# Fusion kernel, 16 batches: the 14 middle batches written out one by one, in place of a loop of 14 passes

## The reference, cut to what matters

```
h = concat(x @ W_tok + position_table, text_embedding(x_txt))   # 1024 + 77 rows of 128
y = layernorm(h)
for each of 8 heads (64 wide): q, k, v = y @ wq, y @ wk, y @ wv
    o = softmax(q k^T / 8) v
h = h + concat(o) @ head_kernel
f = layernorm(h) * ln_scale + ln_bias
out = h + shared_ffn(f) + sum over the 2 chosen of 8 experts (weight_e * expert_e(f))
```

## Time and profile before

| | |
|---|---|
| median of 3 runs | 4751.49 us |
| the profiled execution | 4757.83 us |
| its span, first to last instruction | 4756.0 us |
| instructions | 93178 |
| PE busy | 4492.7 us, 94% |
| DVE, ACT, POOL busy | 68%, 48%, 62% |
| mean granted TensorE clock | 0.979 |

### The profile page before, as it was taken

How to read it: one execution, slowest core, us unless ns; L and a number is a source line. 1 busy time by engine, 2 the same in 40 slices (tenths; PEclk the granted TensorE clock), 3 DMA queues, 4 the chain that set the end, 5 groups by cost and what they waited for, 6 DMA issues and landing times.

```text
span 4756.0 us, 93178 instructions
## 1 busy us (share of the span) xinstructions
PE 4492.7 (94%) x26597; PEld 3327.0 (70%) x26597; DVE 3214.1 (68%) x7726; ACT 2300.4 (48%) x5640; POOL 2948.3 (62%) x1803
## 2 busy tenths in 40 slices
PE   5999999999999999999999999999999999999996
PEld 3667767677676776767677676776767777677765
DVE  5557667676675776667676675776667676676744
ACT  2555545445544545545545444555445455454441
POOL 0776666666666666666666666666666666666661
PEclk7999999999999999999999999999999999999998
DMA  2111111111101111111111111011011111111000
GB/s 52 34 33 40 31 30 39 36 28 33 43 26 39 29 32 41 29 34 39 33 31 33 34 34 39 25 33 44 24 39 38 30 34 33 31 37 38 19 19 18
DMA packets 157061, 159.01 MB, mean 33 GB/s; under 512 B 66576, under 2 KB 148359, under 8 KB 156551
## 3 DMA queue, kind: packets, MB, share of 16 engines
q1 hardware_dynamic: 156551, 152.68, 13.2%
HBM read 59.63 MB, written 19.65 MB: 17 GB/s over the span
## 4 chain that ended last, share of the span: by engine, by line
PE 77%; DMA 7%; issue 5%; DVE 4%; ACT 3%; POOL 2%; SPq 1%; DVEq 0%; ACTq 0%; POOLq 0%
PE o_ps L791 21%; PE work L688 12%; PE scores L772 11%; PE scores L774 10%; PE work L747 8%; PE work L680 4%; DMA q_b<-max_rows 4%; DMA sums<-inverse_rows 2%; PE work L708 2%; PE work L699 2%; PE work L731 2%; PE work L736 1%; DMA inverse_rows<-inv_cols 1%; ACT probs L877 1%; DVE part_max L935 1%
## 5 line engine op out<-in xcount | busy, mean ns | idle before, releaser
L1165 POOL TENSOR_TENSOR sums<-sums,probs 128x736 f32<-128x736 f32 (+3 forms) x1344 | 2363.2, 1758 | 840.4 <-ACT probs L877 783.1
L877 ACT ACTIVATE probs<-scores 128x368 f32<-128x368 f32 (+3 forms) x3456 | 1460.3, 475 | 1595.9 <-PE scores L774 1535.4
L935 DVE TENSOR_REDUCE part_max<-work 128x1 f32<-128x368 f32 (+3 forms) x3456 | 1655.9, 530 | 448.8 <-PE work L688 438.5
L772 PE MATMUL scores<-q_a,k_a 128*128 128x368 f32 (+3 forms) x3456 | 1193.9, 345 | 143.3 <-DMA q_b<-max_rows 62.7
L791 PE MATMUL o_ps<-probs,values 128*64 128x368 f32 (+1 forms) x6912 | 1224.8, 490 | 1.5 <-ACT probs L877 0.2
L774 PE MATMUL scores<-q_b,k_b 128*128 128x368 f32 (+3 forms) x3456 | 1146.0, 332 | 0.0
L688 PE MATMUL work<-k_a,q_a 128*128 128x368 f32 (+3 forms) x3456 | 928.5, 352 | 8.8 <-DMA q_a<-q_b 8.1
L791 PEld LDWEIGHTS o_ps<-probs,values 128*64 128x64 f32 (+1 forms) x6912 | 453.8, 139 | 541.1 <-issue 449.2
L772 PEld LDWEIGHTS scores<-q_a,k_a 128*128 128x128 f32 (+1 forms) x3456 | 635.5, 184 | 269.8 <-issue 128.1
L688 PEld LDWEIGHTS work<-k_a,q_a 128*128 128x128 f32 (+1 forms) x3456 | 594.7, 185 | 234.3 <-issue 209.2
L774 PEld LDWEIGHTS scores<-q_b,k_b 128*128 128x128 f32 (+1 forms) x3456 | 638.8, 185 | 17.4 <-issue 4.2
(11 more groups left out here) (183 smaller groups left out, 4499.2 us busy)
## 6 DMA issues: line engine op xcount, KB each, us to landing
sums<-inverse_rows SPq DMA_DIRECT2D x192, 184.0 KB
k_a<-k_a SPq DMA_DIRECT2D x128, 184.0 KB, 2.7
q_a<-q_b SPq DMA_DIRECT2D x128, 184.0 KB, 2.7
k_a<-k_a SPq DMA_DIRECT2D x64, 183.0 KB, 2.7
q_a<-q_b SPq DMA_DIRECT2D x64, 183.0 KB, 2.7
resid_rows<-heads_t SPq DMA_DIRECT2D x16, 576.0 KB, 6.1
h_out<-resid_rows SPq DMA_DIRECT2D x16, 576.0 KB, 8.2
heads_t<-in_pe_table_dram SPq DMA_DIRECT2D x16, 512.0 KB
```

Of the source, the lines that this page charges most:

```text
L772: nc.tensor.matmul(o, k_a[p % 2][i][:, t * P:t * P + n], q_a[p % 2][i][:, c0:c0 + cw], start=True, stop=False)
L877: nc.scalar.activation(probs[0:n, slot(s), i, 0:cw], scores[0:n, h % SB, 0:cw], ACT.Exp, scale=DH ** -0.5).then_inc(probs_ready, 1)
L935: nc.vector.tensor_reduce(part_max[0:n, i * IMG + j if j < IMG else 2 * IMG + i, c:c + 1], w[0:n, 0:keys], AX.X, ALU.max).then_inc(drained ...
L1165: nc.gpsimd.tensor_tensor(acc, acc, probs[0:n, slot(s), :, 0:cw], ALU.add).then_inc(sums_done, 1)
```

## The change

In `run`, the hardware loop becomes a Python loop. The middle 14 batches stand in each engine's stream one after the other, b is an integer in all of them, so the waits of these batches are on constants, and the counting, comparing, branching and register arithmetic fall away. The work, its order on each engine and all buffers stay.

```
         iteration(pro, 0, -1)
         iteration(first, 0, 0)
-        with eng.Fori(1, B - 1) as b:
+        for b in range(1, B - 1):
             iteration(loop, b - 1, b)
         iteration(last, 0, B - 1)
         iteration(epi, 0, B)
```

## The result

The changed kernel takes 4717.7 us, the median of 5 runs (4715.6 to 4730.7), against 4752.3 (4749.5 to 4755.1, 5 runs) for the one before on the same chip: 0.9933 of its time, 95% interval 0.9921 to 0.9944. It is 34.6 us faster where 19.7 were forecast. The profiled execution took 4715.6 us, its span 4713.6. All runs behind the medians here are in the same state but one, a slow run of the last experiment (9373 us), which is left out.

The account below looks back on a forecast made before the run. The prediction took TensorE, busy 94% of the span, and its pauses as the bound. Passages -34.3 us and constants +14.6 us summed to -19.7 us, from 4751.5 to 4732 us; overall range 4705 to 4754 us.

Parts of the forecast that it names:

- The 13 pauses at the branch: TensorE's waits for "issue" when the loop branches back, 43.6 us together, 3.35 us each, would go.
- Rival E: Between batches: the pause isn't the branch's and remains in another form; only +14.6 us stay, 4766 us; chance 0.03.
- The passage's value, 14.50: Each of 13 passages between batches falls from 17.14 to 14.50 us, copy late, clock falling one in three: 34.3 us saved.
- rival B: Passages between batches: the q_a copy isn't late, all go like that into batch 1; -43 us, 4708 us; chance 0.13.
- C: Passages between batches: the copy is late and the clock falls each time; -5 us, 4746 us; chance 0.18.
- Register arithmetic at nothing: On all five engines, removing the loop's register operations gains nothing, since the engines' queues cover them.
- Rival G: Second half of a batch: removing register arithmetic gains back what constants cost there; -34.3 us alone, 4717 us; chance 0.04.
- Constants, 1.04 us a batch,: ScalarE's separate semaphore waits hand exponentials over 0.08 us later: 1.04 us a batch, 14.6 us for 14 batches.
- The doubling: The 0.52 us lost over 49 steps doubled to 1.04 us for a whole batch, whose other half couldn't be compared.
- Steps 53 to 55 unchanged: TensorE's step 53 pause, about 2.1 us, clock falling in 3 of 15 batches, got no term in the sum.
- Rival D: ScalarE's separate waits ahead of exponentials cost more than the branches, from 2.45 us a batch; +26 us, 4778 us; chance 0.09.
- Rival F: Straight-line batches: the instruction stream can't keep up, 267 us for some 230 exposed blocks; 4999 us; chance 0.03.

Follow-up runs that it names:

- the last experiment: The loop kernel before the change, with ScalarE's wait for scores_ready written ahead of those for probs_used and sums_done: 1.0109, 4807.2 us.
- The kernel of two passes: Against the kernel before: loop kept on every engine, but of 2 passes with 7 batches written out in each, registers kept: 0.9950, 4725.3 us.
- the small load: Against the kernel before: middle batches written out on TensorE only, residual load cut to 32 bytes a partition, h_out zeroed once: 0.9909, 4707.9 us.
- TensorE alone: Against the kernel before: middle batches written out on TensorE only, the other four engines keep the loop: 1.0019, 4759.3 us.
- VectorE, GpSimd and SyncE: Against the kernel before: middle batches written out on these three engines, TensorE and ScalarE keep the loop: 1.0007, 4753.8 us.
- TensorE and SyncE: Against the kernel before: middle batches written out on these two engines, the other three keep the loop: 1.0000, 4753.6 us.
- The reordered waits: The changed kernel with ScalarE's wait for scores_ready written first in its step; against the kernel before 0.9912, 4708.7 us, and again 0.9912, 4708.3 us.
- ScalarE alone: Against the kernel before: middle batches written out on ScalarE only, the other engines keep the loop: 1.0072, 4785.9 us.
- the second time: The changed kernel, unedited, run once more beside the version with reordered waits; against the kernel before 0.9928, 4718.7 us.
- TensorE and ScalarE alone: Against the kernel before: middle batches written out on these two engines, the other three keep the loop: 1.0015, 4755.8 us.

## Why the prediction was right, and where it was not

*The 13 pauses at the branch* were right: the 13 waits for "issue" and the branch rows are gone, with the lower clock that followed them. The two windows that the prediction shows for that clock, 0.81, are among the five lowest; in the other eight it was 0.90. The trace of the kernel before also shows what a pause holds. In each of the 13, one 16 KB packet of the instruction fetch on q8 starts 0.9 to 1.6 us behind the start of TensorE's branch and ends at 1.9 to 2.6; the branch that falls through has none. The window of the branch into batch 14, 4082.42 to 4086.13, of the view of the DMA queues:

```profile
q8 instruction: 1, 0.02, 2.2%
```

By the Trainium skill, "Runtime: NRT & Kernel Launch", section "Instruction fetch mechanics", a taken branch out of the fetched window waits for a fetch of the target's code; the packets agree. Rival E (4766) falls.

*The passage's value, 14.50, failed.* It was 12.47, so 4.66 a passage were saved instead of 2.64, 26 us in 13. The step that failed is "I take the wait as there, since batches 2 to 14 follow a batch with feed-forward and output store, as batch 15 does and batch 1 doesn't". I read the passage into batch 15 as a sample of the changed kernel, and it was none for two reasons. Its tail, the end of batch 14, is loop code with registers; with constants everywhere the residual load goes out 0.64 us earlier against the same matmul. And its load was the slowest of the 16, 9.5 us, where I took the median, 8.2, for it; into batch 15 it takes 9.4 us in the changed kernel too, in the 13 others 8.0 to 8.2. With both gone the copy is in time, or late by 0.42 us at most. The kernel of two passes shows the forecast's passage, 13.87, where the tails keep their registers; the small load shows that it is the load that holds the copy up. Mechanism and place of the danger were right, that it would be met was not: this part went as rival B had it (4.45 a passage), and C (4746) falls. That the time still lay in the range is in part luck: the passages gave 26 us more than forecast, and 13 us of costs that the forecast had too low took half of it back.

*Register arithmetic at nothing* holds for the body: about 0 in the steps of the kernels with TensorE alone and with VectorE, GpSimd and SyncE. Rival G falls. Not at the passage: there the tails' register code is worth 1.40 us a passage through the load. No one engine has it all. Into batch 15, where all these kernels have a straight passage, the load goes out at +0.01 us with every tail on registers, at +0.03 with TensorE written out, at +0.08 with VectorE, GpSimd and SyncE, at -0.24 with TensorE and SyncE, at -0.30 with ScalarE, with or without TensorE, and at -0.64 only with all five.

*Constants, 1.04 us a batch,* had the right mechanism and too small a size: 18.9 / 13 = 1.45 us. The reordered waits show the mechanism, ScalarE alone shows the engine. The doubling was at fault: the first half cost (1.7 + 4.6) / 13 = 0.48, near the 0.52 taken, but the second (6.8 + 5.8) / 13 = 0.97, twice as much. Why isn't shown: TensorE's waits for exponentials, at L772 and L791 together, rose by about as many in the first half (192 in 13 batches) as in the second (187).

*Steps 53 to 55 unchanged*, a term that the sum left out without a word, failed. The three steps cost 0.59 us a batch more: in batches 2 to 14 the clock fell in 4 (3 the second time) instead of 1, and in two batches TensorE's pause itself was 3.0 and 3.2 us in place of 2.1. Why, and whether the constants have to do with it, isn't shown. With passages and constants this makes -60.6 + 18.9 + 7.7 = -34.0, where the same terms of the forecast for 13 batches are -34.3 + 13.5 = -20.8.

*Rival D* (more than 2.45 us a batch) falls by its own mechanism, the constants' 1.45. Its sign, that a batch without its passage grows by more than 2.4 us, came near: 26.6 / 13 = 2.05, for the falls at steps 53 to 55 are in it. With TensorE and ScalarE alone it was 36.5 / 13 = 2.8, and the kernel was slower than before. *Rival F* falls: it needed 267 us.

Open: why the load into batch 15 takes longer than the others, and about half of the 8.4 us at the ends of the span, which lie in batches 0 and 15, where both kernels have the same code.

## What to carry to other kernels

A boundary that a trace seems to show "already unrolled" is a sample only if both sides of it are unrolled, and one sample needs its own rows: compare its transfer with the others before taking their median for it. Look at the code that issues the transfers, not only at the engine that pauses. Removing a pause on the bounding engine is worth only what the next transfer allows; here that hung on one load on a shared queue, its issue and its length. Of the variants that wrote out only some engines and computed everything, none was faster than the loop. When an instruction has more waits than it can hold, look at which wait the compiled instruction carries, and try an order in which it is the one that ends last. The same edit that gained 10 us with constants cost 56 in the loop.

## What the runs showed of the hardware

- A taken branch back over a long body cost TensorE 3.5 us at the median, with one 16 KB instruction packet on q8 inside it each time; to take away VectorE's, GpSimd's and SyncE's gained nothing (1.0007). The Trainium skill, "Advanced Engine Details and Errata", section "Control Flow Timing", has about 108 ns for a compare-and-branch; TensorE's taken ones took 30 times that here, VectorE's 63 ns, and the measurement decides.
- A separate semaphore instruction of 38 ns, if it holds the wait that ends last, delays the exponential behind it by 0.08 us; the register operations in its place by 0.15.
- The pause at steps 53 to 55 is 1.8 to 3.2 us in all kernels, mostly 2.1. In batches 2 to 14 the clock fell there in 1 batch before, in none with VectorE, GpSimd and SyncE written out, in 4 and 3 in the two runs of the changed kernel, and in 5 to 12 in all others, at some 1.5 to 2 us each; there these steps cost 11 to 19 us in all. In the first run of the changed kernel it didn't fall at the two longest pauses, 3.0 and 3.2 us, but at five shorter ones of 2.1 to 2.6. What decides it isn't shown.
- The same 576 KB load took 8.0 to 8.2 us into batches 2 to 14 of the changed kernel, 8.7 to 9.4 in the straight passages of the two passes, and 9.4 and 9.6 into batch 15 in the two runs of the changed kernel.
